# Attention scores from two fp32r parts, even and odd heads on opposite halves of TensorE's rows

## The reference

```python
def _L0_attn_ref(x, Wqa, Wqb, Wkva, Wkvb, Wout, bout):      # H, KVH, D = 16, 4, 16
    q = (x @ Wqa @ Wqb).reshape(b, s, H, D)
    kv = (x @ Wkva @ Wkvb).reshape(b, s, KVH, D, 2)
    k, v = (kv[..., 0], kv[..., 1])
    q = _rope(q)
    k = _rope(k)
    k = jnp.repeat(k, H // KVH, axis=2)
    v = jnp.repeat(v, H // KVH, axis=2)
    scores = jnp.einsum('bqhd,bkhd->bhqk', q, k) * D ** (-0.5)
    scores = jnp.where(causal[None, None], -jnp.inf, scores)
    out = jnp.einsum('bhqk,bkhd->bqhd', softmax(scores), v).reshape(b, s, E)
    return out @ Wout + bout
x = x + _L0_attn_ref(_layernorm(x, axis=-1), ...)
x = x + _L0_xattn_ref(_layernorm(x, axis=-1), ctx_1024, ...)
x = x + _L0_ffn_ref(_layernorm(x, axis=-1), ...)
```

## Time and profile before

| | us |
|---|---|
| median of the runs | 1352.33 |
| fastest run | 1351.51 |
| the profiled execution | 1347.93 |
| its span | 1346.2 |
| PE busy in the span | 1057.0 (79%) |
| DVE busy | 783.6 (58%) |
| ACT busy | 661.9 (49%) |
| POOL busy | 342.8 (25%) |

### The profile page before, as it was taken

How to read it: one execution, slowest core, us unless ns; L and a number is a source line. 1 busy time by engine, 2 the same in 40 slices (tenths; PEclk the granted TensorE clock), 3 DMA queues, 4 the chain that set the end, 5 groups by cost and what they waited for, 6 DMA issues and landing times. The chain is left out here.

```text
span 1346.2 us, 22491 instructions
## 1 busy us (share of the span) xinstructions
PE 1057.0 (79%) x6813; PEld 764.0 (57%) x6813; DVE 783.6 (58%) x1685; ACT 661.9 (49%) x1166; POOL 342.8 (25%) x524
## 2 busy tenths in 40 slices
PE   3766068788999984892566999999998999998875
PEld 2444023343444433772454877878787787877764
DVE  4888356576777743864344664746556474655523
ACT  1334115466666673461224456473755747364433
POOL 0443136566333331010111120403012040301200
PEclk9777558899999996896677999999999999999987
DMA  2332423333222103357102030301203030020000
GB/s 85 106 113 78 133 87 119 105 117 113 91 88 96 58 33 128 133 224 265 47 12 98 1 125 0 109 16 40 84 0 115 10 109 16 0 78 1 15 1 16
DMA packets 52156, 103.20 MB, mean 77 GB/s; under 512 B 6584, under 2 KB 31936, under 8 KB 48000
## 3 DMA queue, kind: packets, MB, share of 16 engines
q1 hardware_dynamic: 48924, 95.02, 20.6%
q0 software_dynamic: 1920, 6.03, 1.4%
q10 hardware_dynamic: 1252, 1.39, 0.3%
HBM read 62.45 MB, written 39.58 MB: 76 GB/s over the span
## 5 line engine op out<-in xcount | busy, mean ns | idle before, releaser
L804 ACT ACTIVATE p_probs<-p_psS 128x512 f32<-128x512 f32 (+1 forms) x352 | 180.7, 564 | 121.5 <-ACTq L803 119.1
L706 DVE CUSTOM_DVE_ANT_0 p_psA<-p_psA,p_mask 128x512 f32<-128x512 f32 (+1 forms) x256 | 155.6, 647 | 103.5 <-DVEq L704 103.1
L1744 DVE TENSOR_TENSOR p_hl<-p_h,p_hh 128x512 fp32r<-128x512 f32 x128 | 86.9, 688 | 156.2 <-DVEq L1743 154.2
L838 PE MATMUL p_psA<-p_ks,p_qs 96*128 96x512 bf16 (+3 forms) x512 | 144.1, 317 | 36.7 <-PEq L836 36.4
L857 PE MATMUL p_psS<-p_qs,p_ks 99*128 99x256 bf16 (+3 forms) x512 | 130.6, 308 | 19.6 <-PEq L882 11.3
L1629 ACT ACTIVATE p_h<-p_psG,w_columns 128x512 f32<-128x512 f32 x128 | 88.2, 689 | 100.3 <-ACTq L1628 99.9
L868 PE MATMUL p_psO<-p_probs,p_v 128*32 128x512 f32 (+3 forms) x1024 | 92.2, 454 | 27.5 <-PEq L864 26.8
L725 POOL TENSOR_SCALAR_AFFINE_SELECT p_probs<-p_probs 128x512 f32<-128x512 f32 x128 | 80.6, 634 | 129.6 <-POOLq L724 112.4
L1597 POOL TENSOR_TENSOR p_base<-p_x,p_q 128x1024 f32<-128x1024 f32 x8 | 20.0, 2502 | 363.1 <-POOLq L1596 352.9
L1955 PE MATMUL p_psY<-p_n,p_hh 128*128 128x256 f32 x512 | 105.8, 290 | 2.7 <-PEq L2015 2.3
L857 PEld LDWEIGHTS p_psS<-p_qs,p_ks 99*128 99x128 bf16 x512 | 43.6, 98 | 105.7 <-issue 90.7
(11 more groups left out here) (247 smaller groups left out, 2750.7 us busy)
## 6 DMA issues: line engine op xcount, KB each, us to landing
p_n<-n_parts SPq DMA_DIRECT2D x16, 1024.0 KB, 6.7
o_sums<-p_o SPq DMA_DIRECT2D x32, 256.0 KB, 2.9
n_parts<-p_nh SPq DMA_DIRECT2D x8, 1024.0 KB, 3.9
n_parts<-p_nl SPq DMA_DIRECT2D x8, 1024.0 KB, 6.0
q_parts<-p_part SPq DMA_DIRECT2D x48, 128.0 KB
p_qs<-q_parts SPq DMA_DIRECT2D x32, 192.0 KB
p_x<-in_x_dram SPq DMA_DIRECT2D x8, 512.0 KB, 3.9
p_qs<-q_parts SPq DMA_DIRECT2D x32, 128.0 KB
```

The source lines that it names most:

```text
L706: nc.vector.tensor_tensor_reduce(out=bank[:, 0:w], in0=bank[:, 0:w], in1=mask[:, S - w:S], scale=1.0, scalar=MASKED, op0=ALU.add, op1=ALU.max,
L804: nc.scalar.activation(probs[:, g % 2, at:at + n * w], psS[place(s, turn) % SB][:, 0:n * w], ACT.Exp, scale=SCALE).then_inc(exp_done, 1)
L838: last = nc.tensor.matmul(bank[:, z * w:(z + 1) * w], qs[0:SROWS, k, g * G + r0 + z, i * P:(i + 1) * P], ks[0:SROWS, k, g, 0:w], start=Tru ...
L1744: nc.vector.tensor_tensor(hl[:, s, :], h[:, s, :], hh[:, s, :].bitcast(F32), ALU.subtract).then_inc(h_parts, 1)
```

## The change

Queries and keys are kept as two fp32r parts instead of three bf16 ones, and a score is the sum of three products of parts, so 48 rows of the array. The two parts of the maximum take two more rows. Even heads have their rows at partitions 0 to 49 and odd heads at 64 to 113, with the keys in both places. `SUNITS` and `AUNITS` have 12 units each, and a column unit and the row unit behind it are always of opposite halves.

- project_phase: DVE's subtraction at L332 and ACT's copy at L424 go away, and the parts are fp32 wide. There are as many stores as before (three for each unit: the first part of q twice), each of twice the bytes: 256 KB for q, 128 KB for k.
- loads in attend_phase: two DMAs of 48 rows for the queries of a group and two for the keys of two heads, each part at its own rows in DRAM; before, three of 48, 32 and 16 rows, which repeated a part. The bytes of the queries stay (384 KB), those of the keys double.
- The -1 rows are now set in two memsets of fp32 (32 rows x 4096 each) at the very start of the phase on DVE, ahead of everything there, and ACT issues the first keys only after both. `v` lies in a buffer of the later phases.
- The maxima: two operations of POOL instead of four, a transpose in fp32 into the last 128 columns of the bank of column unit 4 (before, a bank of its own), and two DMAs instead of one.
- The mask product of two heads is one matmul of 256 columns, and heads of units j = 2 and j = 3 go in one matmul of 512 and 256 columns.

```diff
-PAIRS = [(0, 0), (0, 1), (0, 2), (1, 0), (1, 1), (2, 0)]
-PARTS = 3
-SROWS = len(PAIRS) * D
-MROWS = 3
+Q_PARTS = (0, 0, 1)
+K_PARTS = (0, 1, 0)
+SROWS = len(Q_PARTS) * D
+MROWS = 2
+HALF = P // 2
...
-        part = [sb(f"part{i}", [P, RING, S], BF16) for i in range(3)]
+        part = [sb(f"part{i}", [P, RING, S], F32R) for i in range(2)]
...
-                        nc.vector.tensor_tensor(rem[0:rows, n], rot[0:rows, n], part[0][0:rows, n],
-                                                ALU.subtract).then_inc(rem_ready, 1)
...
-                        nc.vector.tensor_tensor(part[2][0:rows, n], rem[0:rows, n], part[1][0:rows, n],
+                        nc.vector.tensor_tensor(part[1][0:rows, n], rot[0:rows, n], part[0][0:rows, n].bitcast(F32),
...
-        PV0_AT, PV1_AT = 7, 10
...
-        SUNITS = [(0, r, 1) for r in range(G)] + [(1, r, 1) for r in range(G)] + [(2, 0, 2), (2, 2, 2), (3, 0, 4)]
-        LAST = [3, 7, 9, 10]
...
+        PV0_AT, PV1_AT = 8, 11
...
+        SUNITS = [(0, (0,)), (0, (2,)), (0, (1,)), (0, (3,)), (1, (1,)), (1, (3,)), (1, (0,)), (1, (2,)),
+                  (2, (0, 2)), (2, (1, 3)), (3, (1, 3)), (3, (0, 2))]
+        LAST = [3, 7, 9, 11]
...
-        AUNITS = [(3, 0, 1), (2, 0, 1), (3, 1, 1), (2, 1, 1), (1, 0, 2), (3, 2, 1), (2, 2, 1), (3, 3, 1), (2, 3, 1),
-                  (1, 2, 2), (0, 0, 4)]
...
+        AUNITS = [(3, (1,)), (2, (1,)), (3, (0,)), (2, (0,)), (3, (2,)), (2, (2,)), (3, (3,)), (2, (3,)),
+                  (1, (1, 3)), (1, (0, 2)), (0, (0, 2)), (0, (1, 3))]
...
+            for e in range(2):
+                nc.vector.memset(ks[e * HALF + 32:(e + 1) * HALF].bitcast(F32), -1.0).then_inc(minus_set, 1)
...
-                nc.gpsimd.tensor_tensor(mrem[:, :], rows, hi, ALU.subtract).then_inc(pool_step, 1)
...
+            act.wait_ge(minus_set, 2)
+            act.sem_inc(minus_set, -2)
...
-                for z in range(n):
-                    last = nc.tensor.matmul(bank[:, z * w:(z + 1) * w], qs[0:SROWS, k, g * G + r0 + z, i * P:(i + 1) * P],
-                                            ks[0:SROWS, k, g, 0:w], start=True, stop=(n == 1))
...
+                for z, r in enumerate(heads):
+                    rows = slice(r % 2 * HALF, r % 2 * HALF + SROWS)
+                    last = nc.tensor.matmul(bank[:, z * w:(z + 1) * w], qs[rows, k, (g * G + r) // 2, i * P:(i + 1) * P],
+                                            ks[rows, k, g, 0:w], start=(z == 0), stop=(n == 1))
+                if n > 1:
+                    last = nc.tensor.matmul(bank[:, 0:n * w].rearrange("p (r k) -> p r k", r=n)[:, :, i * P:w], ident_b[:, :],
+                                            mask_b[:, :].unsqueeze(1).broadcast_to([P, n, P]), start=False, stop=True)
```

More of the change, by code:

```diff
@@ L310, in pair @@
             def pair(ahead):
-                for step in range(RING + 3):
+                for step in range(RING + 2):
                     if step < RING:
@@ L396, in pair @@
             def pair(ahead):
-                for step in range(RING + 2):
+                for step in range(RING + 1):
                     if step < RING:
@@ L418, in pair @@
                         transposed(1)
[L419 to L424, removed]
                 if ahead:
@@ L613, in load_keys @@
             two = slice(z * KVH // 2, (z + 1) * KVH // 2)
[L614 to L617, removed]
-                queue.dma_start(ks[rows, k, two].rearrange("p g t -> p (g t)"),
-                                scr["k"][0:n, b, :, two].rearrange("i d g t -> i d (g t)")).then_inc(kv_in[k][z], 16)
-                row += n
+            for e in range(2):
+                queue.dma_start(ks[e * HALF:e * HALF + SROWS, k, two].rearrange("p g t -> p (g t)").bitcast(F32),
+                                scr["k"][:, :, b, two].rearrange("i d g t -> (i d) (g t)")).then_inc(kv_in[k][z], 16)
             queue.dma_start(v[:, k, two].rearrange("p g t n -> p (g t n)"),
@@ L728, in split @@
             def split(g):
-                rows = mx[:, g * G:(g + 1) * G, :].rearrange("p h t -> p (h t)")
-                hi, mid, low = (msplit[:, g, i, :] for i in range(MROWS))
+                rows = mx[:, g * G:(g + 1) * G, :].rearrange("p (r e) t -> p e r t", e=2)
+                hi, low = (msplit[:, g, :, i] for i in range(MROWS))
                 pool.wait_ge(maxima_done, 1)
@@ L846, in maxima @@
                 pe.sem_inc(split_ready, -1)
[L847 to L848 removed]
+                return nc.tensor.transpose(bank[0:MROWS * NG, S - P:S], msplit[:, g].rearrange("p e i r t -> p (e i r t)").bitcast(F32),
+                                           ident[:, :])
             def score_cols(bank, k, g, s):
[L852 to L859 removed]
+                j, heads = SUNITS[s]
+                w, n, e = widths[j], len(heads), heads[0] % 2
+                rows = slice(e * HALF, e * HALF + SROWS + MROWS)
+                first = (g * G + heads[0]) // 2
+                nc.tensor.matmul(bank[:, 0:n * w].rearrange("p (r q) -> p r q", r=n), ks[rows, k, g, j * P:(j + 1) * P],
+                                 qs[rows, k, first:first + n, j * P:S], start=True, stop=True).then_inc(S_ready, 1)
             def values(k, g, j):
@@ L895, in batch @@
                     rows = g + AHEAD < KVH or has_next
-                    pe.wait_ge(m_in[g], 16)
-                    pe.sem_inc(m_in[g], -16)
+                    pe.wait_ge(m_in[g], 32)
+                    pe.sem_inc(m_in[g], -32)
                     for s in range(len(SUNITS)):
+                        bank = ring(s, start)
                         if turn and s == TURN:
-                            maxima(ring(TURN, start), (g + 1) % KVH)
-                        score_cols(ring(place(s, turn), start), k, g, s)
+                            maxima(bank, (g + 1) % KVH)
+                        score_cols(bank, k, g, s)
                         if rows and s in ROWS_AT:
```

130 lines of the change are left out of this document (49 added, 81 removed).

## The result

The changed kernel takes 1469.7 us (four executions, 1464.2 to 1472.0) against 1352.7: 1.086 times as long (95% interval 1.082 to 1.089). One of the four executions of the kernel before took 3423.9 us and stays out of that ratio; the other three lie between 1351.5 and 1353.0. The prediction had 1319, within 1286 to 1348, and gave "slower" a chance of 0.08. Its third rival, PE's clock at the lower level in all 30 groups, had been priced at 1469.

The account below looks back on a forecast made before the run. It took DVE as fullest in the project phase, PE in the attend phase, with POOL sharing the first 12 groups. Terms +6 - 11 - 19 - 9 = -33 from 1347.9 gave 1315, plus 4.4 for the runs' median 1319; range 1286 to 1348.

Parts of the forecast that it names:

- third rival: Attend phase: with less work PE is granted 1.2 GHz; 1379 with 12 groups at the lower clock, 1469 with all 30; chance 0.10.
- The step that failed: Argument against the third rival: from 493 to 507 us PE did less work than a changed group, at clock 1.00.
- The rival's own ground: Support for the third rival in the attend phase: PE's clock was 0.50 while it idled for 8 us.
- Project phase: Phase ahead of attend: ends 6 us later, as doubled stores take 29.5 us a pair against 26.5 of compute.
- Start of the attend phase: From the phase's start to the first column product: 28.9 us instead of 40.4, so -11 us.
- Steady groups and first 12: Attend groups: last 18 at 8.6 us instead of 9.11, -9 us; first 12 in 113.6 instead of 132.6, -19 us.
- halves run side by side: Attend groups: units of opposite halves overlap, each pair lasting as its wider unit, 2.5 us a group instead of 4.3.
- cost of a change of form: Attend groups: each change of tile form on PE costs 0.10 us, six more a group 0.6 us.
- floor of 7.70 for ACT: Attend groups: ACT with its three banks needs about 7.70 us a group, whatever PE saves.
- first rival: Attend groups: halves run one after the other or drains eat the overlap; 9.4 us a group, 1344; chance 0.20.
- the second (stores hidden): Project phase: stores hide behind compute and the phase ends 16 us early; 1297; chance 0.15.

## Why the prediction was wrong

**The step that failed** is the one against the third rival: "from 493 to 507 us PE does only column units and values, and its clock stays 1.00; that is less work than the changed group has". It compared busy times. The column products of that stretch use 99 rows, those of the changed group 48 and 50, and the runs with 48, 64, 66 and 80 rows show that this decides. The rival's own ground was no better: the clock of 0.50 while PE idled had been at that level since 134.9 us, through both groups of row units. So the weight of 0.10 was wrong.

That the rival's price met the result, 1469 against 1469.7, is in part luck. It was the price of 30 groups wholly at the lower clock, 8.6 + 5 = 13.6 us each; the groups took 13.7 with the clock up for a quarter of the time. Wholly at the lower clock they would have taken some 15.5 us (an estimate: the 2.6 us of work in the stretch at the upper clock, doubled, and the 10.2 at the lower), close to the 15.9 of the kernel with one half at a time. The price had left out what masks, turn and changes of form cost more there. For the whole kernel, 10 us too many in the first 12 groups stand against 3 us too few ahead of them, 1 in the steady ones and 6 behind the last copy.

Even the rival's reason ("with less work, PE could be granted 1.2 GHz") was not the mechanism: twice the row products and one half at a time gave PE more to do, and the clock did not stay.

**Project phase**, +6 forecast, +3.3 measured. The mechanism is as forecast: the stores end the phase. The loop of a pair fell to 27.05 us (first rotation products at 60.06 and 87.11 us) against 26.5 forecast and 30.4 before, DVE ends its last subtraction at 130.9, 11 us earlier than before (142.0), and has nothing more to do while the stores run:

```profile
130.26 0.68 DVE L325 TENSOR_TENSOR p_part<-p_rot,p_part 64x512 fp32r<-64x512 f32 x1 [2.29 <-DVEq L324]
155.41 3.47 DVE L676 MEMSET p_ks<- 32x4096 f32 x1 [24.46 <-PEq L111]
```

From 110 to 154 us the queue's packets take 85 ns each (the row below: 46.1% of 16 engines for 44 us, over 3819 packets) against the 88 taken; the share foretold was over 0.5. Twice the bytes ate all that the missing subtraction gave.

```profile
q1 hardware_dynamic: 3819, 7.31, 46.1%
```

**Start of the attend phase**, -11 forecast, -5.2 measured: the first column product comes 35.1 us after the start, forecast 28.9, before 40.4. The memsets took 7.9 us as forecast (they began 0.9 us into the phase). Two terms were too small. The keys, issued from 163.37 on, were there for PE only at 170.45, 7.1 us later, as all first loads now run at once (18 us from 154.5 at 0.9 of 16 engines); the forecast had 5.3 after its 8. And the row units of a group took 8.2 and 8.1 us, not 6.0 and 5.9: most of it in the four units with a mask, on half rows with changes of form around it, which take 4.0 us together, where the three before took 2.0. The clock was at its lower level for both, as it had been before. The maxima did land in time (12 KB, not the 6 of the prediction).

```profile
170.45 1.38 PE L821 MATMUL p_psA<-p_ks,p_qs 48*128 48x512 f32 x4 [46.63 <-PEq L818]
...
181.07 1.44 SPq L626 DMA_DIRECT2D p_qs<-p_mrows  x2
```

**Steady groups and first 12**, -9 and -19 forecast, +81.9 and +30.7 measured. That halves run side by side was right (3 ns between the starts; a pair whose wider product has 512 columns takes 0.43 us at the lower clock, from L821 at 448.30 to 448.72, as one product alone would: 512 columns at 1.2 GHz). The cost of a change of form was taken too low, 0.20 there and back against 0.32. The floor of 7.70 for ACT was right in kind: at the upper clock PE waits for it. What the waits of POOL and the late maxima had cost in the first 12 groups is gone (13.61 us a group there, 13.66 in the steady part), but a group bound by PE at half its clock hides all that. In the kernel with 112 rows, where the clock is up, the first 12 groups take 9.79 on the mean instead of 11.05, 15.2 us less. The 23.3 us that they had lost over the steady pace are gone there altogether, where I had left 10.4 of them; but its steady pace is slower by 0.7 us a group, which gives POOL and the maxima more time too.

The first rival (drains and no overlap) and the second (stores hidden) did not happen. The rule of the Trainium skill that was weighed there, "TensorEngine Tiling (Array Packing)", section "Key Properties", agrees with the runs in both halves: tiles run in parallel, and changing the mode costs time, 0.32 us for a way there and back in the runs here.

## What to carry to other kernels

Before splitting a product over halves of the array, compare not the time PE is busy but the rows that it uses while it is: in this kernel products on 48 to 66 of 128 rows let the clock fall to half for all or most of the time, in bf16 as in fp32r and with no pause between them. A group took 4.6 us more, where the overlap had been forecast to bring 1.8. A look at the granted clock of the kernel before with its slices cut to the new number of rows, a change of a few lines, would have told it. And where another engine's own pace lies close under PE's (7.70 against 9.11 us here), price the change against that engine first.

## What the runs showed of the hardware

- Dense bf16 products on 48 or 64 rows, PE busy for 160 of 160 us: clock 0.50 all the time. On 66 rows: 0.57, in runs of groups at either level; on 80: 0.98; on 96 and 99, and in fp32r on 112: 1.00 (all from 330 to 490 us).
- Filler work on all rows raised the clock by where it stood more than by how much it was: 3072 columns at 12 places 0.96, 6144 columns at six places 0.87, 3072 at six 0.78.
- A change from products on half rows (fp32r) to one on all rows (bf16) costs 0.20 us at the upper clock, the way back 0.12, with the load of the next stationary operand in it.
- A memset of fp32 takes as long as a bf16 one of as many elements, 3.47 us for 32 x 4096; I had bounded it from that row, and it was the bound itself.
- Left open: why products on both halves at once (98 rows in all) held the clock for only a quarter of the time where 99 rows in one product hold it throughout. The changed kernel has pauses at the upper clock, but with the row products doubled PE was busy for 157 of 160 us and the clock still at 0.74; the rows in one tile are few, and no run shows how they are counted.
